# Mamba's dt projections one to a slot and x_proj copied a slot sooner, with the turned half banks of attention shared evenly by ScalarE and VectorE

## Chip, cores, metric

The program runs on one core of a Trainium2 chip (trn2). The metric is the device time of one execution in microseconds; shorter is better. The engines of the core are named here as the profile names them: PE is TensorE (PEld its weight loads), DVE is VectorE, ACT is ScalarE, POOL is GpSimd and SP is the sync engine, which only issues transfers.

## The reference, cut to what matters

The whole network is group norm and a convolution-attention layer, then a bidirectional Mamba with an MLP, then a mixture of eight experts. The change touches the attention and the scan of Mamba:

```python
# layer 0: attention over 4096 positions, 64 channels, for 8 heads (2 images x 4 groups)
scores = jnp.einsum('bgnc,bgmc->bgnm', qf, kf) * (1.0 / math.sqrt(c))
attn = jax.nn.softmax(scores, axis=-1)
ctx = jnp.einsum('bgnm,bgmc->bgnc', attn, vf)
...
# layer 1, _mamba, once forward and once backward; D = 256, DI = 512, DS = DR = 16, K = 4
xz = jnp.einsum('bld,ed->ble', x, in_proj_w)
xc, z = jnp.split(xz, 2, axis=-1)
xp = jnp.pad(xc, ((0, 0), (K - 1, 0), (0, 0)))
xc = sum((xp[:, k:k + Ls, :] * conv_w[:, k] for k in range(K))) + conv_b
xc = jax.nn.silu(xc)
x_dbl = jnp.einsum('bld,ed->ble', xc, x_proj_w)
dt = x_dbl[..., :DR]
Bm = x_dbl[..., DR:DR + DS]
Cm = x_dbl[..., DR + DS:]
dt = jax.nn.softplus(jnp.einsum('blr,dr->bld', dt, dt_proj_w) + dt_proj_b)
A = -jnp.exp(A_log)
dA = jnp.exp(dt[..., None] * A)
dBx = dt[..., None] * Bm[:, :, None, :] * xc[..., None]
# h = dA_t * h + dBx_t ;  y = sum over s of h * C_t
y = ys.transpose(1, 0, 2) + xc * Dp
y = y * jax.nn.silu(z)
return jnp.einsum('bld,ed->ble', y, out_proj_w)
```

## The kernel before

The phases run one after another, each a block in which every engine has its own program, and semaphores order them against each other: convolution, attention (about 370 to 3030 us of the span), tokens, Mamba (about 3200 to 6800 us), MLP, routing, experts, gather.

**Attention** (`attention_phase`). There are 8 heads of 32 query tiles, 256 tiles of 128 queries. A tile goes through four units k = 0 to 3. All five programs go through the same loop, `step(s)` of each engine (PE L575, ACT L620, POOL L654, DVE L698). In unit k TensorE does, in this order: the scores of a pair of 512-wide blocks for a later tile (`scores`, L538; each pair has two halves, on the two halves of the array's rows), between the two halves the wait `may_turn` (L548) that the exponentials are there and that the turned banks of the unit before have been copied out; 16 transposes of probabilities into the two banks of `ps_t` (`transposes`, L553); and the 16 value products of the unit two back (`values`, L562). `turned_half(i)` (L505) numbers the half banks of a tile: i = 2k and 2k + 1 belong to unit k. The lists ON_ACT and ON_DVE (L454) say which engine copies half i from `ps_t` to `p_turned`, and `turned` (L494) derives from them for how many copies of each engine to wait. ScalarE copies its halves first in a unit (L618) and then does an exponential of 1024 columns (L611). VectorE copies its halves (L682), then copies a pair of scores out with their maximum (`copies`, L668), and in unit 2 also ends the tile before (`finish`, L690). GpSimd subtracts the high parts to get the low ones (L652), after both halves of the unit are copied, and in unit 0 copies the next `q_tile` (L646), on which the scores of unit 2 wait.

**Mamba** (`mamba_phase`). The work is 32 steps (16 chunks of 512 positions, for two directions j by turns). A step has 32 slots q, one for each of 16 states of each of two halves of the channels. In slot q VectorE scans two blocks (L1548) and multiplies the result of slot q - 2 by C (L1555), if that slot is one of C_ON_DVE; GpSimd does that product for the others (L1477, slots 3, 5, 7, 9, 15, 17, 19 and 28), and prepares the input of slot q + 3 (L1471). ScalarE makes the decays of slot q + 1 in two instructions (L1339), into three banks that the scans free. TensorE in slot q sums the result of slot q - 4 into `ps_y` (`accumulate`, L1164, eight transposing products at L1175) and then spreads the row of C for slot q - 2 over the partitions into the one bank `ps_c` (`spread_c`, L1155, product at L1162). In slots 4 and 20 the sum comes last instead of first.

Between these, each step also does the projections of the next one. At which slot each engine does which piece is written out by hand (L920 to L926), and each engine executes in program order, so a piece that waits holds up what follows it in its engine's slot and later. The pieces that matter:

- x_proj: TensorE in slots 18 and 19 (PE_XP), ScalarE copies the result twice, to `xf` (L1307) and as bf16 to `xbc` (L1308), in `xp_copy` at slot ACT_XP. `xf[32:64]`, that is B and C, is stored to DRAM by SP (L1069) and loaded again, spread over the partitions (L1077).
- dt: `dt_proj` (L1150) does four products of 16 rows (PE_DT), each in a bank of `ps_p`. ScalarE reads each with two instructions, `dt_parts` (L1314, L1319 and L1320, at ACT_DT), and then frees the bank. `soft` (L1322) makes the softplus of two blocks at a time with Exp (L1324) and Ln (L1326), at SOFT_AT. GpSimd adds and weighs them (L1496, L1500), half 0 in slots 25 and 27, half 1 in slots 0 and 2 of the next step.
- The way back: `back` (L1179) adds the skip product (L1186) and the transposed sums (L1188), in slots 23 and 24 for the first half (PE_BACK). VectorE gates the result in slots 25 and 26 (L1566).
- `ps_p` has two banks, given out by turns in the order of `order` (L930), here: x_proj, dt 0, dt 1, dt 2, dt 3, back 0, back 1. A piece can start when the one two before it has been read and its bank freed (semaphore `p_free`).

```python
for e in range(K):
    if PE_DT[e] == q:
        dt_proj(s, e)
if q in PE_BACK[0]:
    back(s, 0, PE_BACK[0].index(q))
```

The last step has no next one, so the pieces for the next step occur in 31 of the 32.

Of the kernel before, what the change touches and what calls it, by code (L numbers as in the profile page):

```python
# [418 lines left out]
def attention_phase(nc, ctx, ident, q_full, k_full, v_split, attn_out):  # L419
# [31 lines left out]
    LAG = 2  # L451
    scale = 1.0 / 16.0

    ON_ACT, ON_DVE = (0, 2, 4, 5, 6), (1, 3, 7)  # L454
    HALF = PAIR // 2
    Q_AT = 0

# [394 lines left out]
def mamba_phase(nc, ctx, ident, w, u1, m_dirs):  # L852
# [65 lines left out]
    C_ON_DVE = tuple(q for q in range(SLOTS) if q not in C_ON_POOL)  # L918

    PE_CONV, PE_Z, PE_OUT, PE_XP = ((0, 1), (2, 3), (7, 8), (9, 10)), (1, 4, 11, 12), ((13, 14), (16, 17)), (18, 19)  # L920
    PE_DT, PE_X = (21, 21, 22, 22), (26, 27, 28, 29)
    ACT_CONV, ACT_Z, ACT_OUT, ACT_XP = (2, 4, 9, 11), (3, 5, 12, 13), (16, 18), 20
    ACT_DT, ACT_X = (22, 22, 23, 23), (27, 28, 29, 30)
    SILU_AT, PART2_AT, SOFT_AT = 14, 23, (23, 24)
    TAKE_AT, PE_BACK, GATE_AT, FREE_AT = (18, 3), ((23, 24), (5, 6)), ((25, 26), (6, 7)), ((25, 26), (6, 7))
    RES_AT, SPLIT_AT, DTADD_AT, DTX_AT = 22, 24, (25, 0), (27, 2)  # L926
    LENT = 2 * (SILU_AT + 1) + 1
# [1364 lines left out]
def hybrid_kernel(nc, a, out):  # L2292
# [5 lines left out]
    with ExitStack() as whole:  # L2298
# [13 lines left out]
        with ExitStack() as ctx:  # L2312
            attention_phase(nc, ctx, ident, q_full, k_full, v_split, attn_out)
# [5 lines left out]
        with ExitStack() as ctx:  # L2319
            mamba_phase(nc, ctx, ident, {k[8:]: v for k, v in a.items() if k.startswith("L1_attn_")}, u1, m_dirs)  # L2320
# [50 lines left out]
```

## Time and profile before

| | us |
|---|---|
| median of 3 runs | 8098.92 (8095.15 to 8099.15) |
| profiled execution | 8096.61 |
| its span, first to last instruction | 8094.9 |
| mean granted TensorE clock over the span | 0.917 |
| PE busy | 6922.9 (86%) |
| DVE busy | 6010.3 (74%) |
| POOL busy | 5808.5 (72%) |
| ACT busy | 4653.5 (57%) |

Busy times are of the whole span, over stages that differ, so that the shares tell little by themselves. The granted clock is a share of full speed; 1.0 is the 2.4 GHz level and 0.5 the 1.2 GHz level. Times of rows are microseconds from the start of the span.

### The profile page before, as it was taken

How to read it: one execution, taken by the hardware profiler on the slowest of the kernel's cores; microseconds unless marked ns; L12 is line 12 of the kernel's file. 1: busy time of each engine (PE TensorE's matmuls, PEld its weight loads, DVE VectorE, ACT ScalarE, POOL GpSimd, SP SyncE). 2: the span in 40 equal slices, each digit the busy share in tenths (PEclk: the TensorE clock that was granted, in tenths of full speed). 3: DMA queues.
4: the chain of work that ended last, by engine and by line, in shares of the span. 5: the costliest groups of instructions: out<-in, count | busy, mean ns of one | idle time of the engine just before them, and what ended most of it. 6: DMA issues, size and time to landing. Idle time of an engine off the chain costs nothing. (4 is left out here: it accounts for less than half of the span.)

```text
span 8094.9 us, 165843 instructions
## 1 busy us (share of the span) xinstructions
PE 6922.9 (86%) x56132; PEld 5006.7 (62%) x56132; DVE 6010.3 (74%) x8278; ACT 4653.5 (57%) x7795; POOL 5808.5 (72%) x4008
## 2 busy tenths in 40 slices
PE   8799999999999994788888888888888876757993
PEld 6677777777777773455555555555555554546882
DVE  4477777777777774899999999999999996640116
ACT  2377767767777762666666666666666663211223
POOL 0188878878888880899999999999999995321006
PEclk9899999999999996889998999889998987978995
DMA  3301011010110005122221112222212222332113
GB/s 106 104 0 27 0 27 27 0 27 0 27 27 0 6 5 190 67 70 72 72 74 67 61 64 73 70 74 67 69 60 70 71 69 73 133 146 77 63 57 129
DMA packets 175718, 489.50 MB, mean 60 GB/s; under 512 B 31894, under 2 KB 70452, under 8 KB 154160
## 3 DMA queue, kind: packets, MB, share of 16 engines
q1 hardware_dynamic: 158256, 442.45, 16.7%
q10 hardware_dynamic: 10880, 25.28, 0.8%
q0 software_dynamic: 6144, 16.33, 0.6%
q8 instruction: 226, 3.70, 0.2%
q14 instruction: 212, 1.74, 0.1%
HBM read 360.72 MB, written 123.73 MB: 60 GB/s over the span
## 5 line engine op out<-in xcount | busy, mean ns | idle before, releaser
L1548 DVE TENSOR_TENSOR_SCAN hh<-mb_ps_da,state,hh 128x512 f32<-128x512 f32 x2016 | 2447.0, 1262 | 78.4 <-POOL hh L1471 55.3
L1471 POOL TENSOR_TENSOR hh<-dtx,bb 128x1024 f32<-128x1024 f32 x1024 | 2401.6, 2370 | 126.4 <-PE mb_ps_y L1175 118.1
L652 POOL TENSOR_TENSOR p_lo<-p_turned 128x512 bf16<-128x512 f32 x2048 | 2086.3, 1040 | 526.9 <-ACT p_turned L618 270.6
L1339 ACT ACTIVATE mb_ps_da<-dt,amat 128x512 f32<-128x512 f32 x2016 | 1372.3, 685 | 1016.1 <-DVE hh L1548 1000.9
L1175 PEld LDWEIGHTS mb_ps_y<-ident,hh 128*128 128x128 f32 x8192 | 1007.0, 150 | 724.9 <-issue 341.0
L545 PE MATMUL ps_s<-k_head,q_tile 64*128 64x512 f32 x4096 | 1383.0, 643 | 57.6 <-POOL q_tile L663 44.3
L1175 PE MATMUL mb_ps_y<-ident,hh 128*128 128x128 f32 x8192 | 1157.1, 289 | 280.1 <-POOL hh L1477 226.3
L671 DVE TENSOR_SCALAR_CACHE_REDUCE prob<-ps_s 128x1024 f32<-128x1024 f32 x1024 | 1248.0, 1219 | 97.0 <-PE ps_s L545 90.5
L611 ACT ACTIVATE prob<-prob,nmx 128x1024 f32<-128x1024 f32 x1024 | 1169.6, 1142 | 27.5 <-DVE nmx L676 27.5
L618 ACT ACTIVATE p_turned<-ps_t 128x512 f32<-128x512 f32 x1280 | 736.4, 596 | 771.8 <-PE ps_t L558 771.8
L558 PEld LDWEIGHTS ps_t<-ident,prob 64*128 64x128 f32 x16384 | 911.0, 139 | 358.4 <-issue 319.3
L1555 DVE TENSOR_TENSOR hh<-hh,mb_ps_c 128x1024 f32<-128x1024 f32 x768 | 917.8, 1195 | 122.3 <-PE mb_ps_c L1162 121.5
L682 DVE COPY p_turned<-ps_t 128x512 f32<-128x512 f32 x768 | 530.8, 691 | 605.0 <-PE ps_t L558 605.0
L558 PE MATMUL ps_t<-ident,prob 64*128 64x64 f32 x16384 | 888.5, 224 | 5.7 <-issue 5.2
L570 PE MATMUL ps_o<-v,p_turned 128*128 128x128 bf16 x8192 | 849.0, 222 | 3.8 <-POOL p_lo L652 1.9
L571 PE MATMUL ps_o<-v,p_lo 128*128 128x64 bf16 x8192 | 809.0, 193 | 1.8 <-issue 1.8
L570 PEld LDWEIGHTS ps_o<-v,p_turned 128*128 128x128 bf16 x8192 | 699.2, 98 | 75.9 <-issue 3.8
L571 PEld LDWEIGHTS ps_o<-v,p_lo 128*128 128x128 bf16 x8192 | 713.0, 99 | 0.0
L1477 POOL TENSOR_TENSOR hh<-hh,cc 128x1024 f32<-128x1024 f32 x256 | 604.7, 2362 | 33.2 <-ACT state L1348 33.2
L545 PEld LDWEIGHTS ps_s<-k_head,q_tile 64*128 64x128 f32 x4096 | 487.8, 186 | 202.9 <-issue 50.4
L1123 PE MATMUL mb_ps_p<-xpre,cwd 128*128 128x512 f32 x1024 | 535.9, 651 | 42.6 <-ACT xs L1284 23.0
L1162 PE MATMUL mb_ps_c<-xbc,pick 128*128 128x512 bf16 x768 | 322.3, 420 | 257.0 <-DVE hh L1555 255.6
(228 smaller groups left out, 8321.2 us busy)
## 6 DMA issues: line engine op xcount, KB each, us to landing
bb<-mb_bc SPq DMA_DIRECT2D x128, 1024.0 KB, 4.7
cc<-mb_bc SPq DMA_DIRECT2D x256, 256.0 KB, 3.2
q_head<-q_full SPq DMA_DIRECT2D x16, 1024.0 KB, 16.2
mb_u<-u SPq DMA_DIRECT2D x32, 512.0 KB, 4.6
m_dirs<-dtx SPq DMA_DIRECT2D x32, 512.0 KB, 8.3
ex_w<-in_L_ffn_w SPq DMA_DIRECT2D x16, 1024.0 KB, 7.6
xbuf<-ml_zero SPq DMA_DIRECT2D x16, 640.0 KB, 5.5
ex_xr<-xbuf SPq DMA_DIRECT2D x40, 256.0 KB, 2.7
```

What stands on the lines that cost most here:

```text
L545: last = pe.matmul(ps_s[:, p % 2, half, :], qcur[u][rows, :], kf[j][rows, p, :], start=True, stop=True)
L558: last = pe.transpose(ps_t[:, half, m * DH:(m + 1) * DH], prob[s.u][rows, (KB * k + m) * P:(KB * k + m + 1) * P], ident[rows, rows])
L570: pe.matmul(ps_o[:, u, 0:P], his, vv[j][:, KB * k + m, :], start=(k == 0 and m == 0), stop=False)
L571: last = pe.matmul(ps_o[:, u, 0:DH], lo[:, k, m, :], vv[j][:, KB * k + m, 0:DH], start=False, stop=(k == UNITS - 1 and m == KB - 1))
L611: act.activation(prob[u][:, cs], prob[u][:, cs], ACT.Exp, bias=nmx[:, u:u + 1], accum_out=rs[:, u, c:c + 1]).then_inc(exp_ready, 1)
L652: pool.tensor_tensor(lo[:, k, ms, :], pt[:, k, ms, :], hi_view[:, k, ms, 1::2], ALU.subtract).then_inc(lo_ready, 1)
L671: dve.tensor_scalar(prob[u][:, 2 * p * CH:2 * (p + 1) * CH], ps_s[:, p % 2, :, :].rearrange("p a n -> p (a n)"), scale, -FLT_MAX, ALU.mult ...
L1175: last = pe.matmul(ps_y[:, tb // 2, at:at + P], hh[:, r % RING, kk, tb * P:(tb + 1) * P], ident[:, :], start=(r % S == 0 and at == 0), sto ...
L1339: act.activation(decay(s, q, e), dt[:, j, blk, :], ACT.Exp, scale=amat[:, j, blk, r % S:r % S + 1]).then_inc(da_ready, 1)
L1471: pool.tensor_tensor(hh[:, r % RING], dtx[:, j, half(r // S)], bb[:, r % S, :].unsqueeze(1).broadcast_to([P, HK, CH]), ALU.mult).then_inc( ...
L1548: dve.tensor_tensor_scan(h, a, h, state[:, s.j, q % S, blk:blk + 1], ALU.mult, ALU.add).then_inc(scanned, 1)
L1555: dve.tensor_tensor(hh[:, r % RING], hh[:, r % RING], ps_c[:, :].unsqueeze(1).broadcast_to([P, HK, CH]), ALU.mult).then_inc(hc_dve, 1)
```

## The change

Three lists change, and nothing else. In attention, half 5 of each tile (unit 2) is copied by VectorE, no longer by ScalarE, so that in each unit ScalarE copies the even half and VectorE the odd one. In Mamba the copies of x_proj move from ScalarE's slot 20 to 19. The dt projections move on TensorE from slots 21, 21, 22, 22 to 20, 21, 22, 23, and ScalarE's reads of them from 22, 22, 23, 23 to 21, 22, 23, 24. The first softplus moves from slot 23 to 22; the second stays at 24, behind the read of dt 3, which is now in the same slot. The order in which the banks of `ps_p` are given out stays as it was.

```diff
@@ -451,7 +451,7 @@
-    ON_ACT, ON_DVE = (0, 2, 4, 5, 6), (1, 3, 7)
+    ON_ACT, ON_DVE = (0, 2, 4, 6), (1, 3, 5, 7)
     HALF = PAIR // 2
@@ -918,10 +918,10 @@
     PE_CONV, PE_Z, PE_OUT, PE_XP = ((0, 1), (2, 3), (7, 8), (9, 10)), (1, 4, 11, 12), ((13, 14), (16, 17)), (18, 19)
-    PE_DT, PE_X = (21, 21, 22, 22), (26, 27, 28, 29)
-    ACT_CONV, ACT_Z, ACT_OUT, ACT_XP = (2, 4, 9, 11), (3, 5, 12, 13), (16, 18), 20
-    ACT_DT, ACT_X = (22, 22, 23, 23), (27, 28, 29, 30)
-    SILU_AT, PART2_AT, SOFT_AT = 14, 23, (23, 24)
+    PE_DT, PE_X = (20, 21, 22, 23), (26, 27, 28, 29)
+    ACT_CONV, ACT_Z, ACT_OUT, ACT_XP = (2, 4, 9, 11), (3, 5, 12, 13), (16, 18), 19
+    ACT_DT, ACT_X = (21, 22, 23, 24), (27, 28, 29, 30)
+    SILU_AT, PART2_AT, SOFT_AT = 14, 23, (22, 24)
```

## Rows read from the trace of the kernel before

**Rows 1.** Busy time by stretch: PE, PEld, DVE, ACT, POOL; then granted clock, DMA.

```profile
1000.00:3000.00 2000.00, 1983.57 (x27634) 1560.09 (x27634) 1467.22 (x3072) 1416.73 (x2495) 1608.60 (x1728) 1.00 0.06 14
3270.00:6770.00 3500.00, 2928.14 (x13141) 1857.02 (x13141) 3354.29 (x2935) 2299.94 (x3700) 3329.36 (x1464) 0.90 0.20 67
```

**Rows 2.** Waits of attention, 1000 to 3000 us: total, times, longest.

```profile
PEld ps_s L545 <- ACT p_turned L618: 29.8, 183, 0.2
```

**Rows 3.** Timeline of one tile of attention: start, length, engine, operation, idle before.

```profile
1500.19 1.22 DVE L671 TENSOR_SCALAR_CACHE_REDUCE prob<-ps_s 128x1024 f32<-128x1024 f32 x1 [0.21 <-PE ps_s L545]
...
1500.59 0.23 PE L570 MATMUL ps_o<-v,p_turned 128*128 128x128 bf16 x1
...
1500.69 1.09 ACT L618 ACTIVATE p_turned<-ps_t 128x512 f32<-128x512 f32 x2 [1.01 <-PE ps_t L558]
...
1501.80 0.28 DVE L696 SCALAR_TENSOR_TENSOR o_head<-ps_o,rinv,otmp 128x64 f32 x1 [0.18 <-DVE otmp L693]
1501.83 0.18 PEld L545 LDWEIGHTS ps_s<-k_head,q_tile 64*128 64x128 f32 x1 [0.16 <-ACT p_turned L618]
...
1503.38 0.23 PE L570 MATMUL ps_o<-v,p_turned 128*128 128x128 bf16 x1
...
1503.48 0.69 DVE L682 COPY p_turned<-ps_t 128x512 f32<-128x512 f32 x1 [1.40 <-PE ps_t L558]
...
1508.18 0.23 PE L570 MATMUL ps_o<-v,p_turned 128*128 128x128 bf16 x1
...
1508.64 0.29 POOL L646 COPY q_tile<-q_head 128x128 f32 x1
...
1510.92 0.23 PE L570 MATMUL ps_o<-v,p_turned 128*128 128x128 bf16 x1
```

**Rows 4.** Waits of the Mamba stage, 3262 to 6770 us: total, times, longest.

```profile
DVE hh L1555 <- PE mb_ps_c L1162: 119.8, 81, 4.0
```

**Rows 5.** Timeline of VectorE: the outputs of slots 22, 23 and 24 of one step.

```profile
3996.96 1.22 DVE L1555 TENSOR_TENSOR hh<-hh,mb_ps_c 128x1024 f32<-128x1024 f32 x1 [1.02 <-PE mb_ps_c L1162]
...
4003.00 1.22 DVE L1555 TENSOR_TENSOR hh<-hh,mb_ps_c 128x1024 f32<-128x1024 f32 x1 [2.44 <-PE mb_ps_c L1162]
...
4006.50 1.20 DVE L1555 TENSOR_TENSOR hh<-hh,mb_ps_c 128x1024 f32<-128x1024 f32 x1
```

**Rows 6.** Timeline of ScalarE in slots 20 to 23 of the same step.

```profile
3988.41 1.29 ACT L1339 ACTIVATE mb_ps_da<-dt,amat 128x512 f32<-128x512 f32 x2
...
3990.12 0.58 ACT L1308 ACTIVATE xbc<-mb_ps_p 128x512 bf16<-128x512 f32 x1
...
3992.46 0.69 ACT L1339 ACTIVATE mb_ps_da<-dt,amat 128x512 f32<-128x512 f32 x1 [1.18 <-DVE hh L1548]
3993.74 0.30 ACT L1348 ACTIVATE state<-hh,keep 128x4 f32<-128x4 f32 x1 [0.59 <-DVE hh L1548]
...
3995.44 0.67 ACT L1319 ACTIVATE dt<-mb_ps_p,dtb 128x512 f32<-128x512 f32 x1
...
4003.12 1.06 ACT L1324 ACTIVATE dtx<-dtx 128x1024 f32<-128x1024 f32 x1
4004.21 1.15 ACT L1326 ACTIVATE dtx<-dtx,one 128x1024 f32<-128x1024 f32 x1
```

**Rows 7.** Timeline of TensorE in slots 21 to 25 of the same step.

```profile
3989.02 1.09 PE L1175 MATMUL mb_ps_y<-ident,hh 128*128 128x128 f32 x8 [2.29 <-POOL hh L1477]
3990.83 3.77 PE L1123 MATMUL mb_ps_p<-xf,wdt 16*128 16x512 f32 x4 [0.72 <-ACT xbc L1308]
...
4002.75 1.80 PE L1186 MATMUL mb_ps_p<-xs,skipd 128*128 128x512 f32 x2
...
4005.91 1.02 PE L1186 MATMUL mb_ps_p<-xs,skipd 128*128 128x512 f32 x2
...
4008.08 0.38 PE L1162 MATMUL mb_ps_c<-xbc,pick 128*128 128x512 bf16 x1
```

**Rows 8.** Busy time by stretch, as rows 1, over part of the same step.

```profile
3990.60:4004.30 13.70, 13.47 (x28) 6.62 (x29) 10.24 (x10) 10.67 (x19) 12.80 (x7) 0.50 0.63 208
```

## The prediction

> **What bounds the kernel now.** I read the busy time by stretch first, to see which engine is full where the change sits; then the waits of each stage; then the timeline of one tile and of one step. In attention [rows 1] TensorE works 1983.6 us of 2000 at the full granted clock (1.00, the 2.4 GHz level), while VectorE (1467), ScalarE (1417) and GpSimd (1609) have room. So time is won there only where TensorE is late. In the Mamba stretch (second line) VectorE is busy 3354 us of 3500 and GpSimd 3329; TensorE has room but a mean clock of 0.90. Time is won there only where VectorE stands still.
>
> Attention, one tile. TensorE goes through four units, each: half the scores' product for a block, a wait that the turned banks are copied out, the other half, 16 turns, 16 value products. The first value product of a unit marks its beat: 1500.59, 1503.38, (two units) 1508.18, 1510.92 [rows 3]. The units thus take 2.79, twice 2.40 and 2.74 us, for the same work. The 2.79 follows the unit k = 2, whose halves 4 and 5 ScalarE copies one after the other: 1.09 us from 1500.69, to 1501.78; the weights of the second half of the scores start at 1501.83 [rows 3]. Where each engine copies one, VectorE's ends 0.80 after the beat (1503.48 + 0.69 against 1503.38), not 1.19. The wait is there in 183 of 192 tiles [rows 2]. The profile books only 0.16 us for it, but the second half of the scores no longer runs beside the first, and the beat says 0.39. The 2.74 of unit 1 is another wait: q_tile is copied by GpSimd at 1508.64 for 0.29 us [rows 3], and the next scores wait for it.
>
> Mamba, one step of 32 slots. VectorE's product of hidden state and C waits for the row of C that TensorE spreads: 119.8 us in 81 waits over the stage [rows 4]. One step shows where: 1.02 us before the output of slot 22 and 2.44 us before that of slot 23 [rows 5], 3.46 us together, 107 us in the 31 steps that prepare a next one, which is most of the 119.8. The cause is in program order on TensorE: dt projections 0 and 1 stand in slot 21, 2 and 3 in slot 22, each pair 3.77 us long [rows 7], and the sum and spread of the next slot queue behind them. The granted clock was 0.50 (1.2 GHz) from 3990.6 to 4004.3 [rows 8], after TensorE had stood idle 2.29 and 0.72 us [rows 7].
>
> **The change, part by part.**
>
> Half 5 goes to VectorE. No instruction is added: 256 copies of about 0.60 us leave ScalarE, 256 of 0.69 us join VectorE, which has some 2.8 us free in a tile of 10.3. In unit 2 both copies start together; the later ends 0.80 after the beat, as in unit 3, so this unit should beat in 2.40: 0.39 us x 256 tiles = 100 us. Bounds: 0.16 us (what the profile books) gives 41, 0.40 gives 102. I take 0.39, since the units beside it have the same work and no such wait.
> What queues behind the new copy on VectorE: the scores' copy (it began at 1500.19, now after the turned copy) and the end of the tile before. From 1500.19 to 1501.80 + 0.28 they take 1.89 us [rows 3]. Behind a copy that ends at +0.80 they end at +2.6 to +2.7; the next turned bank is ready at about +2.50. It is copied up to 0.1 us late, and TensorE has about 0.05 to spare there. Cost: between 0 and 0.1 us a tile, I take 0.02, 5 us. The freed score bank is not missed: it is needed a unit and a half later. GpSimd starts its subtraction earlier, to no gain. The 0.34 us of unit 1 stay, since q_tile's copy keeps its distance to that beat. Attention: -95 us.
> The Trainium skill speaks against this half: "Perfetto Trace Analysis", Optimizing Scalar/DVE Operations, gives VectorE a higher fixed cost on PSUM (about 125 ns) than ScalarE (about 51 ns). The trace agrees in sign: 0.69 for VectorE's copy against 1.09 for two of ScalarE's. It would matter if the copying engine were full; the wait it removes is larger than the difference.
>
> x_proj copied at slot 19. The two copies no longer stand behind a state copy, the scan it waits for and two decays [rows 6], so xbc should be there near 3988.4, not 3990.7. The store of B and C to DRAM and the bb loads behind it on the sync queue may go earlier; nobody waits for them. ScalarE has slack in slots 19 and 20: its decays wait for scans.
>
> dt projections one to a slot. TensorE's slot 20 now waits for xbc (to 3988.4) with one projection ahead of the sum of slot 16, which GpSimd needs only later. By slot 22 TensorE has two projections, three sums and the spread behind it; at full clock that is half of 3.77 + 3 x 1.09 + 0.38 = 5.5 us [rows 7], so near 3994, and VectorE's output of slot 22 is due at 3996.96 - 1.02 = 3995.94. Both old stalls should go.
> The new wait. TensorE has two projection banks. The first product of the way back (back0, slot 23) reuses the bank of dt 2, which ScalarE now frees in its own slot 23, and the sum and spread that VectorE wants in slot 24 stand behind back0. ScalarE's chain [rows 6], an instruction of 0.69 giving way after 0.6: decay from 3992.46 to 3993.06; dt 0, 1.15; state copy 0.2; two decays 1.2; dt 1, 1.15; half the softplus 1.09 + 1.06; two decays 1.2; dt 2, 1.15: 8.2 us, so 4001.3. Before, dt 2 came ahead of the softplus. Then TensorE runs back0, the sum and the spread: at full clock 4005.91 to 4008.46, 2.55 us [rows 7], at half 5.1 (the skip products took 1.80 against 1.02). VectorE's output of that slot, at 4006.50 before [rows 5], starts at 4003.9 (full) or 4006.5 (half); without any stall it would be 4003.04. Gain of a step: 2.6 to 0 us.
> I take 1.0: TensorE has been idle about 3 us before 4001.3, and after a shorter idle time [rows 7] the low clock came, so most of this stretch runs at half. 31 of the 32 steps have this part: -31 us, between 0 and -80. In the end ScalarE's own lateness (softplus half 1 a slot later) is covered: its dt is used in the next step.
>
> **Sum.** 95 + 31 = 126 us. The profiled execution took 8096.6 us (span 8094.9 and 1.7 around it), 2.3 under the median of the runs. Against the median: 8098.9 - 126 = 7973.
>
> **Rivals.**
> A. Attention gains nothing: VectorE's queue in unit 2 makes the copy of unit 3 late by 0.4 us and TensorE pays there what it saved. For it: 1.89 us stand behind the new copy. Against: only 0.1 is missing by the rows. Time: 8098.9 - 31 = 8068. Chance 0.08.
> B. Slower: the low clock runs from slot 20 to slot 24, since the projections are now spread thin with idle time between them. Decides if the clock is half from 3988.4 on: two projections at 1.9, three sums at 2.1 (twice 1.09) and a spread of 0.6 end at 3998.9, 2.9 us after VectorE's due time, and dt 2, the next sum, dt 3 and back0 (all at half) bring the output of slot 24 to about 4010.3, 3.8 us later than before. 31 x 3.8 = 118 against attention's 95: 8122. Against: the sums between the projections are dense work, and in the step shown TensorE was back at full clock after 4004.3 with such work. Chance 0.07, and a partly low clock lies between this and the forecast.
> The Trainium skill has this as a rule: "Perfetto Trace Analysis", Matmul Optimizations, says the engine scales with utilization, "so it's important that matmuls execute back-to-back in batches"; the change does the reverse with the projections. That the clock is low in [rows 8] agrees, but there the batches were whole.
> C. No new wait: back0 finds its bank free. Then all 3.46 us go, 107 us, and 8098.9 - 95 - 107 = 7897. ScalarE's order speaks against it. Chance 0.10.
> D. The change does less than it says, both waits being replaced at once: about 8095. Chance 0.03.
>
> **How the numbers follow.** The forecast has 0.72. Low end: the full attention gain and the full clock, 8098.9 - 102 - 78 = 7919, rounded in to 7922; this leaves out C. High end: full attention gain with half of B's loss (59 us) is 8063, attention's lower bound with a Mamba of 0 is 8058; I stop at 8040, since both need an end of two bounds. A measurement can tell about 0.2%, 16 us. Faster by more: forecast, A, C and most of the ground between, 0.93. Within: 0.03. Slower: 0.04, the outer part of B.
>
> **What would show it.** After: beats of 2.40 in three of four units and 2.74 in one; the wait of the scores' weights for ScalarE's turned bank gone; VectorE's turned copy of unit 3 starting within 0.1 us of ScalarE's. In Mamba: no wait at the outputs of slots 22 and 23, a wait for the spread at slot 24 of 1 to 3.5 us, and back0's first product starting just after ScalarE's copy of dt 2. Wrong if the wait at slot 24 is missing (C), if slots 22 and 24 both wait (B), or if unit 3 takes 2.7 (A).

## The result and the profile after

The changed kernel takes 8075.2 us in the median against 8099.0 (ratio 0.9974, 95% interval 0.9967 to 0.9980): 24 us less, where 126 were forecast and 7922 was the low end and 8040 the high end of the range. The profiled execution has a span of 8078.7 us. By the traces the first scan of Mamba starts 77.5 us earlier than before (3185.3 against 3262.8 us), so attention has brought 77 of the forecast 95; the last scan starts only 10.5 us earlier (6757.5 against 6768.0), so Mamba has cost 67 us where a gain of 31 was forecast. A faster stage is nearly cancelled by a slower one.

Busy time by stretch after the change (PE, PEld, DVE, ACT, POOL; then granted clock, DMA), to be read against [rows 1]:

```profile
1000.00:2900.00 1900.00, 1878.69 (x26999) 1553.36 (x26994) 1543.35 (x3188) 1292.68 (x2251) 1573.34 (x1688) 0.99 0.06 15
3200.00:6750.00 3550.00, 2965.82 (x13110) 1898.84 (x13107) 3338.69 (x2921) 2294.96 (x3688) 3321.16 (x1460) 0.89 0.20 66
```

VectorE has taken the copies of ScalarE in attention. In the Mamba stretch VectorE works 94.0% of the time, against 95.8% in [rows 1], and the mean clock is a little lower (0.89 against 0.90).

The timeline of a tile of attention after the change, from one beat to the next as in [rows 3]:

```profile
1500.14 0.23 PE L570 MATMUL ps_o<-v,p_turned 128*128 128x128 bf16 x1
...
1502.60 0.23 PE L570 MATMUL ps_o<-v,p_turned 128*128 128x128 bf16 x1
...
1502.71 0.69 DVE L682 COPY p_turned<-ps_t 128x512 f32<-128x512 f32 x1 [0.31 <-PE ps_t L558]
...
1503.54 1.04 POOL L652 TENSOR_TENSOR p_lo<-p_turned 128x512 bf16<-128x512 f32 x1 [0.19 <-DVE p_turned L682]
...
1505.24 0.23 PE L570 MATMUL ps_o<-v,p_turned 128*128 128x128 bf16 x1
...
1507.70 0.23 PE L570 MATMUL ps_o<-v,p_turned 128*128 128x128 bf16 x1
...
1510.16 0.23 PE L570 MATMUL ps_o<-v,p_turned 128*128 128x128 bf16 x1
```

The beats are 2.46, 2.64, 2.46 and 2.46 us. The long unit of 2.79 has gone, and the one that waits for q_tile is a little shorter than 2.74. But the units that nothing hindered took 2.40 before and take 2.46 now. GpSimd starts 0.14 us after the end of VectorE's copy (1503.54 against 1502.71 + 0.69); over the stretch from 1000 to 2900 us the median of this distance is 0.14 us, where it was 0.08 in the kernel before. A tile took 10.33 us before (1500.59 to 1510.92 in [rows 3]) and takes 10.02 now; 0.31 us times 256 tiles is 79 us, which agrees with the 77.

Mamba. The wait of VectorE for the spread row, over the whole stage, against [rows 4]:

```profile
DVE hh L1555 <- PE mb_ps_c L1162: 185.3, 90, 5.3
```

One step of it on VectorE (outputs of slots 22, 23 and 24), to be read against [rows 5]:

```profile
3928.82 1.22 DVE L1555 TENSOR_TENSOR hh<-hh,mb_ps_c 128x1024 f32<-128x1024 f32 x1 [2.30 <-PE mb_ps_c L1162]
...
3933.15 1.22 DVE L1555 TENSOR_TENSOR hh<-hh,mb_ps_c 128x1024 f32<-128x1024 f32 x1 [0.73 <-PE mb_ps_c L1162]
...
3940.05 1.22 DVE L1555 TENSOR_TENSOR hh<-hh,mb_ps_c 128x1024 f32<-128x1024 f32 x1 [3.31 <-PE mb_ps_c L1162]
```

TensorE in the same step, against [rows 7]:

```profile
3919.02 1.83 PE L1123 MATMUL mb_ps_p<-xf,wdt 16*128 16x512 f32 x2 [2.60 <-ACT xbc L1308]
3920.78 3.68 PE L1175 MATMUL mb_ps_y<-ident,hh 128*128 128x128 f32 x16
3924.39 2.07 PE L1123 MATMUL mb_ps_p<-xf,wdt 16*128 16x512 f32 x2
3926.39 1.97 PE L1175 MATMUL mb_ps_y<-ident,hh 128*128 128x128 f32 x8
3928.15 0.63 PE L1162 MATMUL mb_ps_c<-xbc,pick 128*128 128x512 bf16 x1
...
3933.04 2.07 PE L1123 MATMUL mb_ps_p<-xf,wdt 16*128 16x512 f32 x2
3935.04 2.08 PE L1186 MATMUL mb_ps_p<-xs,skipd 128*128 128x512 f32 x2
...
3939.47 0.54 PE L1162 MATMUL mb_ps_c<-xbc,pick 128*128 128x512 bf16 x1
```

ScalarE's copy of x_proj, and the end of its read of dt 2:

```profile
3918.31 0.59 ACT L1308 ACTIVATE xbc<-mb_ps_p 128x512 bf16<-128x512 f32 x1
...
3932.47 0.68 ACT L1320 ACTIVATE dtx<-mb_ps_p,dtb 128x512 f32<-128x512 f32 x1
```

Busy time and clock of that stretch:

```profile
3919.30:3939.80 20.50, 20.50 (x57) 11.74 (x57) 14.40 (x13) 16.50 (x26) 16.56 (x10) 0.50 0.56 196
```

TensorE waits 2.60 us for xbc, then works without a gap for 20.5 us at the 1.2 GHz level (0.50). The step shown is a common one: between 3270 and 6690 us the clock's records have a low stretch of 20.5 us 22 times after the change, and one of 13.7 us 29 times before it. Before, such a stretch lasted 13.7 us [rows 8] and VectorE's waits were 3.46 us; now it lasts 20.5 and they are 6.34. The way back (the skip product) starts at 3935.04, as dt 3 ends; dt 2's bank had been read by 3933.15 (3932.47 + 0.68). So the wait at slot 24 comes from TensorE's own queue here, not from the bank.

### The profile page after: what moved, and what is told of

It reads as the page before. It is cut to its first block and busy times, and to the rows that moved or that the text cites. A ratio compares the mean times of both kernels' runs of the same rounds, so it can differ in the third digit from the quotient of the medians.

```text
span 8078.7 us, 165235 instructions
## 1 busy us (share of the span) xinstructions
PE 6883.5 (85%) x56132; PEld 5084.5 (63%) x56132; DVE 6164.0 (76%) x8534; ACT 4532.2 (56%) x7539; POOL 5813.9 (72%) x4008
## 5 line engine op out<-in xcount | busy, mean ns | idle before, releaser
L1175 PEld LDWEIGHTS mb_ps_y<-ident,hh 128*128 128x128 f32 x8192 | 1077.3, 157 | 667.1 <-issue 360.2
L1175 PE MATMUL mb_ps_y<-ident,hh 128*128 128x128 f32 x8192 | 1233.1, 302 | 210.7 <-POOL hh L1477 155.7
L545 PE MATMUL ps_s<-k_head,q_tile 64*128 64x512 f32 x4096 | 1300.3, 637 | 64.2 <-POOL q_tile L663 45.7
L558 PEld LDWEIGHTS ps_t<-ident,prob 64*128 64x128 f32 x16384 | 939.8, 139 | 278.0 <-issue 145.9
L618 ACT ACTIVATE p_turned<-ps_t 128x512 f32<-128x512 f32 x1024 | 612.6, 598 | 815.9 <-PE ps_t L558 815.9
L682 DVE COPY p_turned<-ps_t 128x512 f32<-128x512 f32 x1024 | 708.4, 692 | 424.0 <-PE ps_t L558 420.2
L558 PE MATMUL ps_t<-ident,prob 64*128 64x64 f32 x16384 | 817.0, 223 | 1.1 <-DVE p_turned L682 0.4
L1123 PE MATMUL mb_ps_p<-xpre,cwd 128*128 128x512 f32 x1024 | 508.3, 621 | 55.8 <-ACT xs L1284 36.1
L545 PEld LDWEIGHTS ps_s<-k_head,q_tile 64*128 64x128 f32 x4096 | 446.5, 185 | 168.3 <-issue 55.9
```

Of the source, the lines that this page charges most:

```text
L545: last = pe.matmul(ps_s[:, p % 2, half, :], qcur[u][rows, :], kf[j][rows, p, :], start=True, stop=True)
L558: last = pe.transpose(ps_t[:, half, m * DH:(m + 1) * DH], prob[s.u][rows, (KB * k + m) * P:(KB * k + m + 1) * P], ident[rows, rows])
L1175: last = pe.matmul(ps_y[:, tb // 2, at:at + P], hh[:, r % RING, kk, tb * P:(tb + 1) * P], ident[:, :], start=(r % S == 0 and at == 0), sto ...
```

## The experiments

Two theories for the time that Mamba lost: **C**, the low clock makes TensorE the bound from slot 20 to 24; **O**, the order in which ScalarE frees the projection banks sets the wait. For attention: whether the 0.06 us a unit come from the form of the waits or from VectorE's fuller queue.

**The two halves apart.** e1_attention_only is the kernel before with this edit; e2_mamba_only is the kernel after with it undone.

```diff
-    ON_ACT, ON_DVE = (0, 2, 4, 5, 6), (1, 3, 7)
+    ON_ACT, ON_DVE = (0, 2, 4, 6), (1, 3, 5, 7)
```

> The attention half alone, Mamba as before. By the two traces the attention stage ends 77 us earlier after the change (Mamba's first scan at 3185.3 against 3262.8 us) and all of that should stay: about 8022 us, 8099 - 77. If instead the earlier end is paid back by a later stage, the time stays near 8075.

> The Mamba half alone, attention as before. The scans take 67 us longer after the change (3505 to 3572 us from the first to the last), so about 8166 us. If the two halves don't add, because the phase of the clock's changes against the steps matters, it lies 20 us or more away from that.

Measured: 8022.4 us (0.9905, 0.9888 to 0.9922) and 8162.0 us (1.0071, 1.0054 to 1.0088). 77 less and 63 more, near both expectations. Together they give 8085, 10 us above the changed kernel.

**The waits of attention.** The helper `turned` waits for ScalarE's copies (`pt_act`) and then for VectorE's (`pt_dve`). e3_attention_waits_swapped is e1 with this:

```diff
-        eng.wait_ge(pt_act, ONE + g * len(ON_ACT) + acts)
         eng.wait_ge(pt_dve, ONE + g * len(ON_DVE) + dves)
+        eng.wait_ge(pt_act, ONE + g * len(ON_ACT) + acts)
```

> Attention half alone, with the two waits of `turned` in the other order: VectorE's copies first, ScalarE's last. After the change all units but one beat in 2.46 us where the unhindered ones took 2.40 before, and TensorE and GpSimd have a semaphore instruction of their own for the later of the two copies. Theory 1 (the form and order of the waits costs 0.06 us a unit): the beat goes back to 2.40 and the time falls by about 3 x 256 x 0.06 = 46 us under the attention half alone, to about 7976. Theory 2 (VectorE's fuller queue costs it): the beat stays 2.46 and the time stays within 5 us of the attention half alone.

Measured: 7983.4 us (0.9857, 0.9841 to 0.9874), 39 less than e1. Its timeline:

```profile
1501.28 0.23 PE L570 MATMUL ps_o<-v,p_turned 128*128 128x128 bf16 x1
...
1501.39 0.69 DVE L682 COPY p_turned<-ps_t 128x512 f32<-128x512 f32 x1
...
1502.16 2.04 POOL L652 TENSOR_TENSOR p_lo<-p_turned 128x512 bf16<-128x512 f32 x2 [0.38 <-DVE p_turned L682]
...
1503.71 0.23 PE L570 MATMUL ps_o<-v,p_turned 128*128 128x128 bf16 x1
```

The beat is 2.43 us here (median over 1000 to 2900 us 2.42), and GpSimd follows VectorE's copy after 0.08 us (1502.16 against 1501.39 + 0.69), not 0.14. VectorE's work is the same as in e1, so the order of the waits alone costs more than half of the 0.06 us: 39 us are 0.038 us for each of 1024 units. What makes up the rest, from 2.42 to 2.40, was not found.

The sequencers' records in the traces, from 1000 to 2900 us, show what changed for GpSimd. VectorE's copy is the later one of the two. In 523 of 729 units of the kernel before, and in all 761 of e3, its semaphore is waited for by GpSimd's instruction itself, and ScalarE's by a sequencer instruction ahead of it; in all 749 of the changed kernel, as of e1, it is the other way round, so that a sequencer instruction has still to end after the later copy. The median distance from the end of VectorE's copy to GpSimd's start is 0.08, 0.08 and 0.14 us in these three. TensorE is less plain: the changed kernel and e3 both have the two waits in one sequencer instruction in most units (603 of 749 and 613 of 761), only in the other order, and the median distance from the copy's end to the next load of weights for the scores is 0.09 and 0.07 us, against 0.05 before. That the beat follows these distances is argued and not shown. Only the two lists differ between the kernel before and e1, so they turned the form round. In the code they make the two counts grow by 4 and 4 a tile where it was 5 and 3; that this is what the compiler goes by was not tested.

**The clock of TensorE in Mamba.** e4_mamba_filler is e2 with two products of 128 rows added where TensorE waits for xbc; they go to the bank that dt 0 overwrites.

```diff
+            def filler(s, n):
+                pe.wait_ge(p_free, ONE + use(s, "dt", 0) + 1)
+                for _ in range(n):
+                    pe.matmul(bank(s, "dt", 0), skipd[:, s.nj, 0, :], xs[:, s.nj, 0, :], start=True, stop=True)
...
+                        if q == 20:
+                            filler(s, 2)
```

> The Mamba half alone, plus two products of 128 rows and 512 columns in TensorE's idle time of slot 20, into the bank that dt 0 overwrites; results are unchanged. Theory C (the low clock makes TensorE late from slot 20 to 24): the granted clock stays at 1.0 there, the projections take about 1 us each, not 2, the waits at slots 22 and 23 go and that at slot 24 shrinks from 3.4 to about 1 us; time 90 us or more under the Mamba half alone, near 8070. Theory O (the order does it: ScalarE frees the bank of dt 2 late): the wait at slot 24 stays above 3 us and the time stays within 30 us of the Mamba half alone.

Measured: 8089.1 us (0.9987, 0.9978 to 0.9997), 73 less than e2, with more work on TensorE. Clock of two stretches of a step:

```profile
3985.00:3994.00 9.00, 7.49 (x34) 3.94 (x34) 9.00 (x9) 6.67 (x13) 9.00 (x5) 1.00 0.32 101
3996.00:4003.00 7.00, 5.81 (x13) 2.47 (x12) 6.06 (x6) 6.88 (x12) 6.67 (x4) 0.50 0.57 188
```

TensorE's timeline:

```profile
3987.55 1.12 PE L1123 MATMUL mb_ps_p<-xf,wdt 16*128 16x512 f32 x2 [0.83 <-ACT xbc L1315]
...
4000.74 2.07 PE L1191 MATMUL mb_ps_p<-xs,skipd 128*128 128x512 f32 x2 [1.19 <-ACT dtx L1327]
```

VectorE's:

```profile
4005.12 1.22 DVE L1562 TENSOR_TENSOR hh<-hh,mb_ps_c 128x1024 f32<-128x1024 f32 x1 [3.06 <-PE mb_ps_c L1167]
```

The clock stays at the 2.4 GHz level from slot 20 until dt 2 in slot 22, the first two projections take 1.12 us each, and the waits at slots 22 and 23 are gone. The one at slot 24 is not (3.06 us): now the way back waits 1.19 us for ScalarE to have read dt 2, and the clock has fallen by then. Neither expectation came true whole: C had a gain of 90 us or more and a wait of about 1 us at slot 24, O a gain of at most 30. Each names one part: the low clock made the waits at 22 and 23, and O's wait at 24 lay hidden behind them, at the place where the prediction had put it.

**The old softplus slot, with that filler.** e5_filler_softplus_later is e4 with:

```diff
-    SILU_AT, PART2_AT, SOFT_AT = 14, 23, (22, 24)
+    SILU_AT, PART2_AT, SOFT_AT = 14, 23, (23, 24)
```

> The Mamba half with the two products in slot 20 (as in the run before), and the first softplus put back to ScalarE's slot 23, behind the read of dt 2. Theory O (order): the bank of dt 2 is free 2.1 us sooner, so the way back starts about 1.2 us sooner (then TensorE's dt 3 ends just before it) and the 3.0 us wait at slot 24 shrinks to 1.0 to 1.8; 40 to 65 us less than 8089. Rival (TensorE at half clock is the whole of the wait at slot 24): no change over 10 us.

Measured: 8070.3 us (0.9965, 0.9952 to 0.9977), 19 less than e4, about half of the low end of what O had (40). TensorE:

```profile
3992.65 2.07 PE L1123 MATMUL mb_ps_p<-xf,wdt 16*128 16x512 f32 x2
3994.65 2.08 PE L1191 MATMUL mb_ps_p<-xs,skipd 128*128 128x512 f32 x2
```

The bank of dt 2 is no longer waited for, but dt 3 at half clock stands right ahead of the way back, and VectorE still waits 2.47 us at slot 24 of this step.

**The same on the kernel before.** e6_before_filler puts the two products at the head of slot 21 of the kernel before; e7_xproj_copy_only changes only ACT_XP there, from 20 to 19.

```diff
+                    if s.front and q == 21:
+                        filler(s, 2)
```

> The kernel before, with two products of 128 rows and 512 columns in TensorE's idle time at the head of slot 21, into the bank that dt 0 overwrites; results are unchanged. Clock theory: the old waits at slots 22 and 23 (3.5 us a step) came from projections and sums at half clock, so with the clock at 1.0 from slot 21 on the first wait goes and the second shrinks to under 1.3 us; 60 to 100 us less, near 8020. Rival (the order of projections and sums made them, at any clock): under 25 us less.

> The kernel before with ScalarE's copies of x_proj in slot 19 and nothing else. TensorE's first pair of projections can start at 4.8 us after the start of slot 19's scans, once the sum of slot 17 is done, not at 5.5. All that follows in the slots 21 to 23 comes 0.7 us sooner at the same clock, so 31 x 0.7 = 22 us less, about 8077. If the idle time now ends earlier or later against the clock's changes, it may be 0 to 40 us less; more time than before is expected by no theory.

Measured: 8089.4 us (0.9991, 0.9982 to 1.0001) and 8093.1 (0.9991, 0.9981 to 1.0001): neither can be told from no change. e6's clock theory (60 to 100 us less) failed, and its rival's bound (under 25) held; e7's main expectation was 22 us less, with 0 to 40 allowed. TensorE in e6:

```profile
3988.30 1.98 PE L1123 MATMUL mb_ps_p<-xf,wdt 16*128 16x512 f32 x4 [0.62 <-ACT xbc L1315]
...
3994.29 3.23 PE L1123 MATMUL mb_ps_p<-xf,wdt 16*128 16x512 f32 x4 [2.77 <-ACT dtx L1327]
```

VectorE in e6, the output of slot 23:

```profile
3999.88 1.22 DVE L1562 TENSOR_TENSOR hh<-hh,mb_ps_c 128x1024 f32<-128x1024 f32 x1 [2.90 <-PE mb_ps_c L1167]
```

The first pair takes 1.98 us, not 3.77, and the wait at slot 22 is gone. But dt 2 cannot start before ScalarE has read dt 0 in its slot 22, so TensorE waits 2.77 us and slot 23 takes what slot 22 gave. The old waits thus had two bounds, the clock and behind it the bank, and lifting the first alone brought next to nothing.

**Projections over more rows.** e9_filler_later_wide (from e5) and e10_mamba_wide (from e2) pad the weights of the dt projections with zero rows, to WR = 64 rows instead of 16. The memset of the padding has a place of its own among the constants (these lines are left out here).

```diff
-    wdt = sb("wdt", [R, 2, K * P])
+    wdt = sb("wdt", [WR, 2, K * P])
...
-                fill(s, ("dt", k), lambda ps: [(ps, wdt[:, s.nj, k * P:(k + 1) * P], xf[0:R, :], True, True)])
+                fill(s, ("dt", k), lambda ps: [(ps, wdt[:, s.nj, k * P:(k + 1) * P], xf[0:WR, :], True, True)])
```

> Mamba half with the two products of slot 20 and the softplus in slot 23, as the run of 8070, and each dt projection over 64 rows instead of 16 (the 48 added weight rows are zero, results are unchanged, the products have the same number and length). What is left there is the wait at slot 24, 2.15 us, behind dt 3, the way back and a sum at half clock. Theory P (projections of few rows let the clock fall although TensorE is busy): the clock stays at 1.0 up to slot 24, dt 3 takes 1.1 us and not 2.07, the wait shrinks to 0 to 0.8 us; 40 to 65 us less, near 8015. Rival (idle time alone decides the clock): within 10 us of 8070.

> The Mamba half alone (8162) with dt projections over 64 rows and nothing else. The idle time of 2.6 us in slot 20 stays, so the clock still falls there; but by theory P it comes back sooner, since the projections between the sums no longer count as rest: low for about 3 to 7 us a step, not 17; 8162 less 60 to 110 us. By the rival (idle time alone decides): within 15 us of 8162.

Measured: e10 8093.0 us (0.9992, 0.9982 to 1.0001), 69 less than e2 by nothing but the rows, as theory P had it (60 to 110); e9 8067.7 (0.9962, 0.9948 to 0.9976), the same as e5, where theory P had 40 to 65 less. The clock of a stretch of 20 us in e9 that holds the slots 19 to 24:

```profile
3977.00:3997.00 20.00, 14.02 (x63) 7.32 (x62) 19.51 (x18) 16.57 (x29) 19.59 (x10) 1.00 0.53 174
```

One of its projections (dt 0, in slot 20), and TensorE, ScalarE and VectorE in e9 a little later, in slots 24 and 25:

```profile
3980.45 1.12 PE L1124 MATMUL mb_ps_p<-xf,wdt 64*128 64x512 f32 x2 [0.83 <-ACT xbc L1316]
...
3997.74 2.08 PE L1192 MATMUL mb_ps_p<-xs,skipd 128*128 128x512 f32 x2 [2.83 <-ACT dtx L1328]
```

```profile
3997.02 0.67 ACT L1328 ACTIVATE dtx<-mb_ps_p,dtb 128x512 f32<-128x512 f32 x1
```

```profile
4002.85 1.22 DVE L1564 TENSOR_TENSOR hh<-hh,mb_ps_c 128x1024 f32<-128x1024 f32 x1 [3.22 <-PE mb_ps_c L1168]
```

The full clock brought e9 nothing, since the next bank wait stood behind it: the second product of the way back needs dt 3's bank, and ScalarE reads dt 3 only in slot 24, after the softplus. TensorE stands idle 2.83 us for it, and then works at half clock again (2.08 us).

**That read sooner.** e13_dt3_read_sooner is e9 with the edit below. e15_order_alone is e2 with the edit and the softplus of e5, that is the change's lists in a better order and nothing done about the clock.

```diff
-    ACT_DT, ACT_X = (21, 22, 23, 24), (27, 28, 29, 30)
+    ACT_DT, ACT_X = (21, 22, 23, 23), (27, 28, 29, 30)
```

> As the run of 8068 (products in slot 20, softplus in slot 23, 64 rows), with ScalarE's read of dt 3 in slot 23, ahead of the first softplus. There the clock was back (dt 3 in 1.12 us, 4.2 us low in the slots 19 to 25) and a new wait of 1.7 us stood at slot 25: the second product of the way back started only at 20.4 us, after ScalarE had read dt 3 at 20.3. Theory O (the banks are freed too late): the read of dt 3 ends near 16, the wait at slot 25 goes, and at most 0.7 us of wait for a decay comes in slot 25; 30 to 50 us less, near 8025. Rival (the waits at 24 and 25 have another source): within 10 us of 8068.

> The Mamba half alone with nothing added to TensorE, but with ScalarE's old places for dt 2, dt 3 (both in slot 23) and the first softplus (slot 23). Theory C (at half clock TensorE's own queue from slot 20 to 24 is the bound): the way back waited there for dt 3 and not for a bank, so the time stays within 20 us of 8162. Theory O alone: 40 us or more less.

Measured: e13 8037.3 us (0.9922, 0.9907 to 0.9937), 30 less than e9; e15 8156.8 (1.0059, 1.0036 to 1.0082), 5 from e2. TensorE in e15:

```profile
4008.38 2.07 PE L1123 MATMUL mb_ps_p<-xf,wdt 16*128 16x512 f32 x2
4010.38 2.08 PE L1186 MATMUL mb_ps_p<-xs,skipd 128*128 128x512 f32 x2
```

e13 is at the low end of what was expected (30 to 50 less), and e15 within the 20 us of theory C. With the clock low, the softplus and the read of dt 3 in better places are together worth nothing that can be told (e15); with the filler, the first brought 19 us (e5 against e4), and with the wide projections as well the second brought 30 (e13 against e9). The two largest waits of VectorE that are left in e13, over 3420 us:

```profile
DVE hh L1564 <- ACT state L1356: 36.8, 22, 2.3
DVE hh L1564 <- PE mb_ps_c L1168: 28.9, 29, 4.1
```

The first is the state copy of slot 24, which stands behind the softplus, and now behind the read of dt 3 as well; in e9 these waits were 10.0 us in all. Once more a wait takes the place of another.

**Together.** e8_attention_and_filler is e3's attention with e6's Mamba, e11_attention_swap_mamba_e5, e12_attention_swap_mamba_e9 and e14_attention_swap_mamba_e13 are e3's with the Mamba that they name.

> The attention half with the swapped waits, Mamba's lists as before, and the two products of slot 21. If the parts add: 7983 less what the products bring to the kernel before, that is 7983 - 80 = about 7903 (range 7880 to 7960).

> The attention half with swapped waits, and the Mamba half with the two products of slot 20 and the softplus in slot 23. If the parts add: 7983 - (8099 - 8070) = 7954.

> As the run before, with projections over 64 rows. If the parts add and theory P holds: 7954 less 40 to 65, near 7900. By the rival: 7954.

> The attention half with swapped waits together with this Mamba. If the parts add: 7983 - (8100 - 8025) = about 7908 (range 7890 to 7955).

Measured: e8 7975.9 us (0.9846, 0.9829 to 0.9862), e11 7957.9 (0.9828, 0.9811 to 0.9844), e12 7953.0 (0.9817, 0.9801 to 0.9833), e14 7921.7 (0.9776, 0.9763 to 0.9790). Each is within 10 us of the sum of its parts as measured, so e8's miss is e6's, and e12's is e9's; e11 and e14 came within 14 us of what was expected. e14 beats the kernel before by 2.2% and the changed one by 153 us.

## Why the prediction was wrong

- **The wait in unit 2 of attention.** Right in place and mechanism: the unit went from 2.79 to 2.46, and with the waits in the other order to 2.43. VectorE's queue behind the new copy cost nothing visible, where 5 us were forecast (its copies start with ScalarE's in the tile shown); rival A fell.
- **"This unit should beat in 2.40".** The mis-sized term: the units without another wait beat in 2.46, more than half of it by the form of the waits in `turned` (e3). No row of before could price this, and it was not named. 95 forecast, 77 measured.
- **"The 0.34 us of unit 1 stay".** They did not: this unit went from 2.74 to 2.64, and 0.10 us times 256 tiles are 26 us that the prediction put at nothing. So it is partly luck that 77 is as near to 95 as it is, and this is why e3 gets 116, more than the upper bound of 102. Why the unit is shorter was not followed.
- **x_proj at slot 19.** Times in a step are compared from an origin, the start of slot 19's scans: 3985.3 before, 3915.9 after. xbc ended at 3918.9, 3.0 us after it, where 3.1 had been worked out (3988.4). Right, and worth nothing that can be told by itself (e7).
- **"At mostly full clock: near 3994".** This is the step that failed. The clock fell after TensorE had waited 2.60 us for xbc, and stayed at half for 20.5 us. Slot 22's spread ended 12.9 us after the origin, not 8.7, and the waits at slots 22 and 23, forecast to go, were 2.30 and 0.73 us. The prediction had a row for it, 2.29 and then 0.72 us of idle time before the low stretch in [rows 7], and by its own working TensorE stands idle about 2.6 us in slot 20 (from the spread's end at 3985.85 to xbc at 3988.4); it gave this no price. The sums between the projections did not keep the clock up. That the clock was the cause is shown by two runs that change little else: e4 (73 us) and e10 (69 us).
- **The new wait at slot 24.** Forecast 0.9 to 3.5 us, taken near 2.5, measured 3.31. The bank was the right mechanism only with the clock restored: in e4 the way back starts at 4000.74, 16.3 us after the origin (there 3984.5), where the working gave 16.0. In the changed kernel TensorE's queue got there first.
- **Sum for Mamba.** -31 forecast, +67 by the traces and +63 by e2: about 2.1 us a step. In the step shown the output of slot 24 starts 24.2 us after the origin, against 21.2 before. That is rival B's mechanism at a little over half of its price of 3.8 a step. It had a chance of 0.07, against a row that spoke for it; its sign, that slots 22 and 24 both wait, is what the trace shows.
- **Slips in the sums.** Rival B's terms (3988.4 + 3.8 + 6.3 + 0.6) give 3999.1, not 3998.9, and the low end takes 78 us where 31 x 2.6 are 81. Nothing hangs on either.
- **The rule of batches.** In the steps shown the low stretch was 13.7 us before and 20.5 after. The page "Perfetto Trace Analysis" of the Trainium skill, Matmul Optimizations, asks for matmuls back-to-back in batches; it spoke against the spread, and this kernel agrees. The same page's fixed costs for copies out of PSUM (Optimizing Scalar/DVE Operations), higher for VectorE, did not decide: the copy takes 0.69 us on VectorE and 0.60 on ScalarE, and attention gained.

## What to carry to other kernels

When a trace shows work at half clock, price a reordering at both clocks and look first at the idle time it leaves ahead of that work: here a wait of 2.6 us was followed by 20.5 us at half clock, and two products put into it bought 73 us with the new lists, but only 10, not to be told from none, with the old ones. Several waits in a row may hide each other (clock, bank, read of the next bank, state copy), so that mending one alone shows nothing; change one at a time, but judge the order with the first bound already removed. And when two semaphores are waited for in a tight loop, try both orders: 39 us lay in two swapped lines here, and on GpSimd the faster order was the one in which the instruction itself waits for the later semaphore.

## What the hardware showed beyond what was expected

- Two pairs of kernels differ only in whether the dt projections have 16 or 64 rows: e2 and e10, e5 and e9. At full clock such a projection takes 1.12 us either way (e4, e9). But the mean granted clock over Mamba (3270 to 6690 us) was 0.89 in e2 and 0.91 in e10, 0.93 in e5 and 0.96 in e9, and e10 is 69 us faster than e2. Idle time alone does not tell the clock either: in the steps shown TensorE stands idle 0.83 us before dt 0 and 0.68 before dt 2 in e5, and the clock falls at dt 2 (dt 3 takes 2.07 us); in e9 it is 0.83 and 0.89, and the clock stays (dt 3 takes 1.12).
- In the changed kernel TensorE was busy for 20.5 us of 20.5 and stayed at half clock all the while. The Trainium skill, "TensorE: Matmul & The Clock Gate", What's actually happening, has the clock follow how busy TensorE has been; busy time as the profile counts it did not tell it here.
- The order and form of two semaphore waits moved the start of GpSimd's instruction from 0.14 to 0.08 us after the copy it waits for (medians of e1 and e3).
